# A routed-expert block on one core: the second routing chain moved to the front of the last stage, places by running sums, six shared blocks first, half-block sums at the end

## The chip, the core and the metric

The kernel runs on one core of a Trainium2 chip. The metric is the device time of one execution in microseconds (us), the median of several runs. The engines are named PE (matrix products), DVE (vector), ACT (activations), POOL (GpSimd) and SP (the queue that issues most transfers).

## What is computed

The input is x of 4096 tokens by 256. One attention layer (16 heads, causal, layer norm and modulation ahead of it) is added to x. Then a layer of experts follows, whose input h is the normalised, modulated x. In short form:

```python
logits = xf @ gate_w.T; scores = sigmoid(logits); sfc = scores + gate_bias
g_scores = top_k(sfc.reshape(n, 4, 4), 2)[0].sum(-1)      # 4 groups of 4 experts
gmask = the 2 best groups of each token
topk_idx = the 4 best experts among these groups; topk_w = their scores / sum * 2.5
y = einsum('nei,ne,ehi->nh', silu(xf@Wg) * (xf@Wu), cw, Wd)   # 16 experts, I = 128
shared = silu(xf @ Ws_g.T) * (xf @ Ws_u.T) @ Ws_d.T           # width 256
x = x + gb * (xf + y + shared)
```

Each token goes to exactly two groups, and in each group the kernel computes all four experts, with weight 0 for those not chosen.

## The kernel before

Four stages follow one another, each a block of code that all engines enter together: `prepare` and `attend` (the attention, about 1.65 ms), `project` (output projection, layer norm, router logits, from about 1655 to 1763 us) and `experts` (from 1763 us on).

**Routing.** Tokens are handled in two halves of 16 tiles of 128 (QT = 16). For each half a chain of small DVE instructions runs: `choose` (L1113) finds the two best groups (`mask`, kept as `chosen`) and the expert weights; `count_places` (L1168) lets PE count, by products with a triangular matrix (`earlier`) and a matrix of ones (`every`), how many earlier tokens chose each group, 17 products in all; `place_rows` (L1178) turns the counts into a row of a list for each token and group. `tile_table` (L1191) then works out which group each of the 19 tiles of 512 rows belongs to. Each instruction of a chain waits for the one before. The first half's chain runs inside `project`, one or two instructions at a time between the others (`route`); the second half's chain runs at the start of `experts`.

**Lists.** POOL sends each token's row (normalised input, 16 weights, slot numbers, 1104 bytes) to its two lists in memory by indirect transfers of 128 rows (`scatter`, L1216): 32 for the first half, then, once `s_rows` says the second half's places are there, 32 more.

**The last stage.** `experts` works through a list of jobs: 8 shared blocks S0 to S7 (512 tokens each, two items, one per half of the shared width) and 19 routed tiles R0 to R18 (512 list rows each, four items, one per expert). With FIRST_S = 4 the order is S0 to S3, R0 to R18, S4 to S7. An item is 12 products `up` (L1477) into hg and hu, ACT's silu (`sg`, L1549), DVE's product (L1652), ACT's rounded high part `ahi` (L1553), DVE's remainder `alo` (L1656), and 6 products `down` (L1495) into ya. Around them, per job: PE turns the rows (`turn`, L1443), ACT takes the high part (`high`, hhi, L1529), DVE the remainder (`low`, hlo, L1572); at the end ACT collects ya into z (`collect`, L1538), PE turns it back (`back`, L1458) and DVE takes it (`take`: L1607 for a shared block, L1610 into yo for a tile, which POOL then sends to `yr` by four indirect transfers, L1402). turn, back and the turning of the weights share one PSUM tile `tp`, whose uses have a fixed order, the list `uses`; the counting of places uses it too, as ("L", 0). For shared blocks DVE also runs `begin` (L1595, L1599: the row is gated and the residual added), which overwrites the row that POOL sent, and so waits for `s_sent`. For tiles, the weights of each expert come back from memory, broadcast (`cwb`, L1341), and DVE multiplies hu by them (L1649).

**Order around the change.** SP's queue issues the loads in program order. `load_tile(0)` waits for all scatters to have landed and for `begin` of the last leading shared block (`s_pre`). At the end, the two list results of each token (`yr`, 2 KB per token) are loaded by blocks (`load_pair`, 1 MB each, two buffers in turn: the space of cwb and that of wst) and added by DVE (`combine`, L1616 and L1618), three times inside the shared blocks S5 to S7 and five times after them; each finished block is stored (512 KB, `store`).

## Time and profile before

| | |
|---|---|
| median of 3 runs | 2344.61 us |
| lowest, highest of them | 2327.98, 2355.11 us |
| profiled execution, its own time | 2361.33 us |
| its span in the trace | 2359.1 us |
| PE busy in the span | 2107.5 us, 89% |
| DVE busy | 1763.8 us, 75% |
| ACT busy | 1421.5 us, 60% |
| POOL busy | 503.0 us, 21% |
| mean granted clock of PE | 0.93 |

Times in the text are from the start of the span. A row of the timeline gives the start, the duration, the engine, the line and the operation, output and inputs, the count, and in brackets how long the engine had been idle before it and what released it ("issue": nothing that the profile shows; "remote": a source that the profile doesn't know). A row of the windows view gives the stretch, its length, the busy time and count of each engine, PE's granted clock (1.00 is 2.4 GHz), the busy share of the 16 DMA engines and the GB/s moved. A row of the chain gives start, duration and the piece of work that the next piece waited for.

### The profile page before, as it was taken

The page shows a single profiled execution, that of the slowest core. Times are in us where ns is not written, and L with a number is a line of the kernel's source. Part 1 is how long each engine was busy: PE and PEld are TensorE (multiplying, and loading weights), DVE is VectorE, ACT ScalarE, POOL GpSimd, SP SyncE. Part 2 cuts the span into 40 slices and gives each one's busy share as a digit, 9 for nine tenths or more (in the row PEclk, how much of TensorE's full clock was granted, in tenths as well). Part 3 has the DMA queues.
Part 4 walks back from the last instruction along what each step waited for, and adds up shares of the span by engine and source line. Part 5 has one row for each costly group of instructions (what it writes and reads, how often), then busy time and mean ns, then how long its engine had stood idle before and what let it go on. Part 6 is the DMA issues. An engine that isn't in the chain of part 4 may idle for free. (4 is left out here: it accounts for less than half of the span.)

```text
span 2359.1 us, 43618 instructions
## 1 busy us (share of the span) xinstructions
PE 2107.5 (89%) x17400; PEld 1107.4 (47%) x17400; DVE 1763.8 (75%) x2226; ACT 1421.5 (60%) x2766; POOL 503.0 (21%) x756
## 2 busy tenths in 40 slices
PE   7589999999999999999999999999873689999994
PEld 5233333443444444344444333333573467777773
DVE  6478799999998878899999787764564346566666
ACT  5235577788888877778888888887210233333331
POOL 2000001110111001111101100000416446666640
PEclk9757799999999999999999999999765799999997
DMA  6815011114211111511101110000642233333326
GB/s 228 231 28 84 24 33 38 36 61 60 60 51 43 34 41 44 87 31 52 47 29 40 61 36 23 13 11 2 225 180 101 83 94 112 111 110 98 102 89 231
DMA packets 120685, 180.76 MB, mean 77 GB/s; under 512 B 15665, under 2 KB 80178, under 8 KB 119714
## 3 DMA queue, kind: packets, MB, share of 16 engines
q1 hardware_dynamic: 111776, 154.45, 23.2%
q0 software_dynamic: 6720, 19.01, 2.2%
q10 hardware_dynamic: 1986, 4.51, 0.5%
q8 instruction: 137, 2.24, 0.4%
q14 instruction: 66, 0.54, 0.1%
HBM read 99.92 MB, written 77.60 MB: 75 GB/s over the span
## 5 line engine op out<-in xcount | busy, mean ns | idle before, releaser
L775 DVE TENSOR_REDUCE mx<-S 128x2 f32<-128x1024 f32 (+3 forms) x1152 | 1279.3, 1134 | 200.3 <-PE S L688 127.0
L756 ACT ACTIVATE prob<-ST 128x512 f32<-128x512 f32 (+3 forms) x2304 | 1168.6, 559 | 353.4 <-PE ST L709 308.5
L723 PE MATMUL O<-prob,V 128*17 128x256 f32 (+1 forms) x8704 | 687.7, 389 | 0.3 <-POOL prob L666 0.3
L688 PE MATMUL S<-K,Q 48*128 48x512 f32 (+3 forms) x2304 | 570.2, 493 | 33.3 <-DVE mx L775 22.1
L709 PE MATMUL ST<-Q,K 49*128 49x512 f32 (+3 forms) x2304 | 491.9, 423 | 36.4 <-ACT prob L756 30.9
L688 PEld LDWEIGHTS S<-K,Q 48*128 48x128 f32 x2304 | 223.7, 191 | 472.0 <-issue 300.4
L666 POOL TENSOR_SCALAR_AFFINE_SELECT prob<-prob 128x512 f32<-128x512 f32 x128 | 81.2, 635 | 1208.1 <-ACT prob L756 1208.1
L709 PEld LDWEIGHTS ST<-Q,K 49*128 49x128 f32 x2304 | 223.7, 190 | 137.8 <-ACT prob L756 104.9
L723 PEld LDWEIGHTS O<-prob,V 128*17 128x17 f32 x8704 | 145.6, 96 | 287.1 <-issue 277.9
L1553 ACT ACTIVATE ahi<-sg 128x512 fp32r<-128x512 f32 x92 | 58.2, 632 | 192.5 <-DVE sg L1652 191.6
L1549 ACT ACTIVATE sg<-hg 128x512 f32<-128x512 f32 x92 | 55.4, 603 | 184.1 <-PE hu L1477 159.9
L1656 DVE TENSOR_TENSOR alo<-sg,ahi 128x512 fp32r<-128x512 f32 x92 | 82.5, 897 | 68.1 <-ACT ahi L1553 62.9
L1649 DVE TENSOR_TENSOR hu<-hu,cwb 128x512 f32<-128x512 f32 x76 | 53.1, 699 | 87.8 <-PE hu L1477 44.1
L1477 PE MATMUL hg<-hhi,wst 128*128 128x512 f32 x304 | 110.3, 404 | 0.0
L1495 PE MATMUL ya<-ahi,wst 128*128 128x512 f32 x304 | 109.8, 402 | 0.0
L1477 PE MATMUL hu<-hhi,wst 128*128 128x512 f32 x304 | 106.0, 389 | 0.0
L1402 POOL DMA_INDIRECT yr<-yo,idt x76 | 75.5, 993 | 41.1 <-DVE yo L1610 26.1
L1652 DVE TENSOR_TENSOR sg<-sg,hu 128x512 f32<-128x512 f32 x92 | 63.1, 686 | 21.4 <-ACT sg L1549 9.4
L694 PE MATMUL S<-maskh,idh 64*128 64x128 bf16 x1024 | 78.4, 234 | 0.0
L1219 POOL DMA_INDIRECT lists<-big,rows x64 | 63.0, 985 | 56.7 <-issue 46.3
L1386 POOL CAST wst<-whi 128x512 fp32r x76 | 47.4, 624 | 98.9 <-PE hu L1477 98.1
L1458 PE MATMUL tpe<-identf,z 128*128 128x128 f32 x216 | 30.4, 287 | 37.8 <-DVE hlo L1572 36.6
(235 smaller groups left out, 1804.8 us busy)
## 6 DMA issues: line engine op xcount, KB each, us to landing
cwb<-cwt SPq DMA_DIRECT2D x76, 256.0 KB, 5.3
lists<-wbd SPq DMA_DIRECT2D x132, 138.0 KB, 2.2
Q<-qs SPq DMA_DIRECT2D x192, 64.0 KB, 2.4
xs<-lists SPq DMA_DIRECT2D x19, 552.0 KB, 4.0
K<-ks SPq DMA_DIRECT2D x18, 512.0 KB, 15.3
qs<-hl SPq DMA_DIRECT2D x16, 512.0 KB, 4.3
ks<-hl SPq DMA_DIRECT2D x16, 512.0 KB, 4.2
wraw<-in_wcat SPq DMA_DIRECT2D x54, 128.0 KB, 2.1
```

The costliest lines, as they stand in the source:

```text
L666: pool.affine_select(out=tri, in_=tri, compare_op=ALU.is_ge, fill=0.0, base=0, pattern=[[0, HG], [1, P]], channel_multiplier=-1).then_inc( ...
L688: ins = pe.matmul(out[:, ab, 0:w], Q[g, n % QR, p, r * P:(r + 1) * P], K[G % 2][g, p, c * BW:c * BW + w], start=True, stop=not diag)
L694: ins = pe.matmul(out[:, ab, r * P:(r + 1) * P], idh[g, h, :], maskh[g, h, :], start=False, stop=h == 1)
L709: pe.matmul(ST[(u + ab) % ST_BANKS][:, c0:BW], K[G % 2][g, p, k * P:(k + 1) * P], Q[g, n % QR, p, c0:BW], start=True, stop=True).then_inc( ...
L723: ins = pe.matmul(O[32 * a:32 * a + VC, c0:c1], V[:, G, k, VC * a:VC * (a + 1)], prob[:, s % NP, a, c0:c1], start=s in FIRST and h == 0, s ...
L756: act.activation(prob[:, s % NP, 2 * p + ab, c0:BW], ST[u % ST_BANKS][:, c0:BW], ACT.Exp).then_inc(s_exp, 1)
L775: dve.tensor_reduce(mx[:, n % 2, a:a + step + 1:step, c], S[slot % S_RING][:, :, 0:w], AX_X, ALU.max).then_inc(s_free, 1)
L1402: pool.indirect_dma_start(d["yr"], bass.IndirectOffsetOnAxis(ap=idt[:, r % 4, i:i + 1], axis=0), yo[:, i, :], None).then_inc(s_sc, 16)
L1477: ins = pe.matmul(bank[:, :], w[:, c0:c0 + I], h[:, q % 2, half, :], start=(m == 0), stop=(m == 5))
L1495: ins = pe.matmul(ya[:, half, :], w[:, half * P:(half + 1) * P], a[:, it % 2, :], start=(k == 0 and m == 0), stop=(last and m == 2))
L1652: dve.tensor_tensor(sg[:, it % 2, :], sg[:, it % 2, :], up, ALU.mult).then_inc(s_pr, 1)
L1656: dve.tensor_tensor(alo[:, it % 2, :], sg[:, it % 2, :], ahi[:, it % 2, :].bitcast(F32), ALU.subtract).then_inc(s_act, 1)
```

## The change

- `count_places` issues two products instead of 17: one gives the count within a tile of 128, one the sum of each tile. `place_rows` forms the running sums of these on DVE in four steps (a copy and an addition each), adds the carry, and keeps the next carry; `choose` no longer sums the mask, and signals it right after its comparison.
- In `experts` the second routing chain comes first on DVE and PE: DVE runs `choose` and `place_rows`, then low(0), then `tile_table`, then low(1); PE counts the places before it turns S0. The use ("L", 0) of `tp` stands first, so turn(0) waits until `place_rows` is done.
- FIRST_S is 6: S0 to S5, R0 to R18, S6, S7.
- ACT rounds the next job's rows (`high(q+1)`) before it collects the results of the last job (`collect(q-1)`).
- `combine` and `load_pair` work on half blocks (2 tiles of 128, 512 KB), with six buffers in turn instead of two (cwb twice, wst three times, yo once), and all 16 halves are summed after the last `take`.

```diff
@@ choose
-    yield dve.tensor_scalar(mask, grank, float(TG) - 0.5, None, ALU.is_lt)
-    yield dve.tensor_reduce(r["added"], mask.rearrange("p t e -> p e t"), AX_X, ALU.add)
-    dve.tensor_tensor(r["carry"][:, g + 1, :], r["carry"][:, g, :], r["added"], ALU.add).then_inc(s_mask, 1)
+    dve.tensor_scalar(mask, grank, float(TG) - 0.5, None, ALU.is_lt).then_inc(s_mask, 1)
+    dve.wait_ge(s_mask, 1)
...
@@ count_places
-    pe.matmul(out, r["earlier"], mask, start=True, stop=False)
-    for i in range(1, QT):
-        pe.matmul(out[:, i * NG:QT * NG], r["every"], mask[:, 0:(QT - i) * NG], start=False, stop=False)
-    return pe.matmul(out.rearrange("p (t e) -> p t e", e=NG), r["every"],
-                     r["carry"][:, g, :].unsqueeze(1).broadcast_to([P, QT, NG]), start=False, stop=True)
+    pe.matmul(out[:, 0:QT * NG], r["earlier"], mask, start=True, stop=True)
+    return pe.matmul(out[:, QT * NG:2 * QT * NG], r["every"], mask, start=False, stop=True, skip_group_check=True)
@@ place_rows
-    yield dve.tensor_tensor(place, places.rearrange("p (t e) -> p t e", e=NG), r["first_row"], ALU.add)
+    yield dve.tensor_copy(a, sums)
+    step = 1
+    while step < QT:
+        dve.tensor_copy(b[:, 0:step, :], a[:, 0:step, :])
+        yield dve.tensor_tensor(b[:, step:QT, :], a[:, step:QT, :], a[:, 0:QT - step, :], ALU.add)
+        a, b = b, a
+        step *= 2
+    carry = r["carry"]
+    dve.tensor_tensor(carry[:, g + 1, :], carry[:, g, :], a[:, QT - 1, :], ALU.add)
+    yield dve.tensor_tensor(place, within, r["first_row"], ALU.add)
+    yield dve.tensor_tensor(place[:, 1:QT, :], place[:, 1:QT, :], a[:, 0:QT - 1, :], ALU.add)
+    if g:
+        yield dve.tensor_tensor(place, place, carry[:, g, :].unsqueeze(1).broadcast_to([P, QT, NG]), ALU.add)
...
-FIRST_S = 4
+FIRST_S = 6
+HALVES = 2 * NB
...
-    uses = [("T", 0)]
+    uses = [("L", 0), ("T", 0)]
...
-        yab = [cwb[:, :, :], wst[:, 0:TPB * 2 * D].bitcast(F32).rearrange("p (i n) -> p i n", i=TPB)]
+        yab = [cwb[:, 0:2, :], cwb[:, 2:4, :]]
+        yab += [wst[:, i * 4 * D:(i + 1) * 4 * D].bitcast(F32).rearrange("p (i n) -> p i n", i=2) for i in range(3)]
+        yab += [yo[:, :, :].rearrange("p i n -> p (i n)").rearrange("p (i n) -> p i n", i=2)]
+        ring = len(yab)
...
@@ sync engine
-                load_pair(0)
-                load_pair(1)
-                load_block(FIRST_S + 2)
+                for h in range(ring):
+                    load_pair(h)
                 for b in range(NB):
+                    for h in range(2 * b + ring, min(2 * b + ring + 2, HALVES)):
+                        load_pair(h)
                     store(b)
...
@@ tensor engine
+                need("mask", s_mask, 1)
+                count_places(pe, t, 1, counted).then_inc(s_tp, 1)
                 need("w0", t["s_w"][0], 16 * 4)
                 turn(0)
...
@@ scalar engine
                     if k == 0:
+                        if 0 < q < len(jobs) - 1:
+                            high(q + 1)
                         if q:
                             collect(q - 1)
-                        if 0 < q < len(jobs) - 1:
-                            high(q + 1)
...
@@ vector engine
-                low(0)
-                low(1)
                 for ins in choose(dve, t, 1, s_mask):
                     link(ins)
...
-                        if kind == "S" and x > FIRST_S:
-                            combine(combined)
-                            combined += 1
                 take(len(jobs) - 1)
-                for b in range(combined, NB):
-                    combine(b)
+                for h in range(HALVES):
+                    combine(h)
```

DVE at the start of the last stage, before (hlo is low(0) and low(1), cwb the space of the routing chain):

```order
L1563 UNCONDITIONAL_BRANCH
L1572 TENSOR_TENSOR hlo<-tpe,hhi 128x512 x4
L1118 MEMSET cwb 128x16 x4
L1120 TENSOR_TENSOR cwb<-cwb 128x256
L1125 TENSOR_TENSOR cwb<-cwb 128x16x8
```

And after the change, where the chain has given its rows (L1197, L1198) and the table begins (L1205):

```order
L1194 TENSOR_REDUCE cwb<-cwb 128x16
L1195 TENSOR_TENSOR cwb<-cwb 128x16
L1197 CAST rows<-cwb 128x16
L1198 CAST rows<-cwb 128x16
L1577 TENSOR_TENSOR hlo<-tpe,hhi 128x512 x2
L1205 TENSOR_TENSOR cwb<-cwb 128x32
```

low(0) has moved from before the chain to behind its rows, and low(1) to behind the table.

ACT at the first item of a job, before (hhi is the rounding of the next rows, z the collected results):

```order
L1553 ACTIVATE ahi<-sg 128x512
L1538 ACTIVATE z<-ya 128x512 x2
L1529 ACTIVATE hhi<-tpe 128x512 x2
L1549 ACTIVATE sg<-hg 128x512
L1553 ACTIVATE ahi<-sg 128x512
```

And after the change, at the same place:

```order
L1558 ACTIVATE ahi<-sg 128x512
L1534 ACTIVATE hhi<-tpe 128x512 x2
L1543 ACTIVATE z<-ya 128x512 x2
L1554 ACTIVATE sg<-hg 128x512
L1558 ACTIVATE ahi<-sg 128x512
```

The two pairs have changed places; nothing else moved on ACT but the order of the jobs.

SP's queue at the end, before (xs<-x loads the residual of a shared block, yr holds the list results):

```order
L1317 DMA xs<-x 128x4x256 x2
L1348 DMA cwb<-yr 128x4x512
L1348 DMA wst<-yr 128x4x512
L1317 DMA xs<-x 128x4x256
L1353 DMA out<-big 128x4x256
L1348 DMA cwb<-yr 128x4x512
L1317 DMA xs<-x 128x4x256
```

And after the change:

```order
L1329 DMA xs<-x 128x4x256 x2
L1360 DMA cwb<-yr 128x2x512 x2
L1360 DMA wst<-yr 128x2x512 x3
L1360 DMA yo<-yr 128x2x512
L1360 DMA cwb<-yr 128x2x512 x2
L1365 DMA out<-big 128x4x256
L1360 DMA wst<-yr 128x2x512 x2
```

Six half-block loads now stand in a row, and no residual load stands between the pairs.

## Rows read from the trace of the kernel before

**Rows 1.** Windows of the last stage.

```profile
1763.00:1814.00 51.00, 20.84 (x76) 17.71 (x76) 16.87 (x95) 4.16 (x6) 31.15 (x32) 0.57 0.28 99
1899.00:2288.00 389.00, 361.17 (x1745) 294.22 (x1746) 232.61 (x340) 137.31 (x246) 230.25 (x364) 0.99 0.33 103
2332.50:2359.00 26.50, 0.00 (x0) 0.00 (x0) 12.55 (x11) 0.00 (x0) 0.00 (x0) 0.53 0.81 272
```

**Rows 2.** Timeline of PE near the end of project: counting, then the last turn.

```profile
1746.39 0.67 PE L1171 MATMUL gl<-cwb 128*128 128x64 f32 x2
1746.85 6.51 PE L1173 MATMUL gl<-cwb 128*128 128x60 f32 x30
...
1753.68 1.91 PE L1053 MATMUL tpx<-identf,big 128*128 128x128 f32 x8
```

**Rows 3.** Timeline of DVE from the end of project into the last stage.

```profile
1747.27 1.67 DVE L1005 SCALAR_TENSOR_TENSOR big<-big,rstd,modB 128x256 f32<-128x256 f32 x4
...
1773.87 0.16 DVE L1118 MEMSET cwb<- 128x16 f32 x4
...
1779.98 1.17 DVE L1148 MAX8 cwb<-cwb 128x8 f32<-128x16 f32 x14
...
1788.02 0.11 DVE L1150 MEMSET cwb<- 128x64 f32 x1 [5.52 <-remote]
...
1808.97 0.17 DVE L1152 MATCH_REPLACE8 cwb<-cwb 128x16 f32<-128x16 f32 x1 [0.61 <-issue]
...
1814.38 0.17 DVE L1188 CAST rows<-cwb 128x16 int32<-128x16 f32 x1
...
1858.59 1.22 DVE L1607 TENSOR_TENSOR big<-big,tpe 128x1024 f32<-128x1024 f32 x1 [13.36 <-remote]
```

**Rows 4.** Timeline of POOL: first and last scatter of each half.

```profile
1763.83 1.23 POOL L1219 DMA_INDIRECT lists<-big,rows  x1 [27.39 <-issue]
...
1803.47 0.96 POOL L1219 DMA_INDIRECT lists<-big,rows  x1 [0.30 <-issue]
1814.88 0.96 POOL L1219 DMA_INDIRECT lists<-big,rows  x1 [10.46 <-DVEq L1634]
...
1855.23 0.96 POOL L1219 DMA_INDIRECT lists<-big,rows  x1 [0.30 <-issue]
```

**Rows 5.** Timeline of PE: first down of the stage, and turn(R0).

```profile
1822.89 0.80 PE L1495 MATMUL ya<-ahi,whi 128*128 128x512 f32 x1 [31.02 <-DVE alo L1656]
...
1876.80 1.97 PE L1443 MATMUL tpe<-identf,xs 128*128 128x128 f32 x8 [3.62 <-DMA xs<-lists]
```

**Rows 6.** Chain of waits at the first tile.

```profile
1873.03 3.72 DMA xs<-lists
```

**Rows 7.** Chain of waits within one routed tile.

```profile
1916.93 1.07 ACT z L1538 x2
1917.99 0.49 ACT hhi L1529
1918.51 0.52 DVE hlo L1572
```

**Rows 8.** Waits of back (L1458), 1890 to 2280 us: total, times.

```profile
  DVE hlo L1572: 29.6, 18
```

**Rows 9.** Timeline of PE: turn(S5) and turn(S6) near the end.

```profile
2283.66 1.03 PE L1443 MATMUL tpe<-identf,big 128*128 128x128 f32 x8
...
2294.43 1.04 PE L1443 MATMUL tpe<-identf,big 128*128 128x128 f32 x8
```

**Rows 10.** Timeline of SP: the first pair load.

```profile
2298.73 0.39 SPq L1348 DMA_DIRECT2D cwb<-yr  x1
```

**Rows 11.** Windows: pair loads, residual load and store together.

```profile
2306.00:2314.00 8.00, 2.78 (x13) 1.95 (x12) 6.00 (x8) 3.06 (x6) 0.00 (x0) 0.98 0.99 319
```

**Rows 12.** Timeline of DVE: the last block's sum; page, part 3: an instruction queue.

```profile
2353.36 1.23 DVE L1616 TENSOR_TENSOR big<-big,wst 128x1024 f32<-128x1024 f32 x1 [2.62 <-DMA wst<-yr]
...
q14 instruction: 66, 0.54, 0.1%
```

67 lines of the change are left out of this document (29 added, 38 removed).

## Prediction

> **What bounds the kernel now.** I first read the slices and the windows by stage, to see where PE is not busy. The change touches only the end of `project` and `experts`. There the windows show three different regimes: a start in which PE is busy 20.8 of 51 us [rows 1], a long middle of routed tiles in which it is busy 361 of 389 us, and a tail of 26.5 us after the last product, in which DVE is busy 12.6 us and the DMA engines 81% [rows 1].
>
> For the start I read the timelines of DVE, POOL and PE side by side. POOL sends 32 scatters at 1.28 us each (31 steps from 1763.83 to 1803.47), then sits idle 10.5 us until the second half's rows are there at 1814.4, and sends 32 more, 1.30 us each, until 1856.2 [rows 3, 4]. The routing chain of the second half starts on DVE at 1773.87, since low(0) and low(1) come first, and takes 40.7 us to its rows at 1814.55. Most of that is not work: it stops at 1781.15 and is back to its pace only at 1808.97 [rows 3]. In these 27.8 us DVE issues 26 small instructions, 1.07 us each, some of them with no wait in them at all. The same happens in the second run of scatters: `take` of S0 starts at 1858.59 after 13.4 us of waiting for nothing that the profile knows, 2.4 us after the last scatter [rows 3, 4]. So in both runs DVE comes nearly to a halt some 17 to 20 us after the scatters begin, and is freed 2.4 to 4.5 us after they end. I call this the standstill. It makes PE wait 31.0 us ahead of its first `down` [rows 5]. What ends last at the start is then this: R0's rows are loaded at 1873.03, land 3.7 us later, and turn(R0) runs at 1876.80 [rows 5, 6]. That time is the milestone of the start.
>
> For the middle I followed the chain of waits: in a tile it goes through z, then hhi, then hlo, then back [rows 7]. `back` waits for hlo 18 times, 29.6 us, 1.64 each [rows 8]. For the tail I read SP's queue and DVE: pair loads begin at 2298.73, when the last rows have been sent, and the last sum starts at 2353.36, after waiting for its load [rows 10, 12].
>
> All sums are made against the profiled execution, 2361.3 us (span 2359.1 and 2.2 around it). The median of the runs shown is 16.7 lower, and I carry that over at the end. A measurement of this kernel can tell about 1%, 23 us, from no change.
>
> **End of project.** Counting takes PE from 1746.39 to 1753.68, 7.3 us for 17 products; two of them take 0.67 [rows 2]. The turn behind it needs DVE's last rows, which end at 1748.94 [rows 3]. The chain's steps shift by two slots, so a long one (16 MATCH_REPLACE) moves ahead of the rows of block 6, which delays PE there, but DVE's total up to the rows of block 7 stays. I put the last turn at 1749.4 instead of 1753.68: **4.3 us** off, bounds 2 and 4.8. The 11 added instructions of `place_rows`, about 0.25 us each, run on DVE while PE does the last logits, and cost nothing as long as they take less than those 7 us. The stage then starts at about 1758.6.
>
> **Start of the last stage.** The chain starts at once. Without the standstill its length is 40.7 less 27.8, 12.9 us, plus about 3 for the sums: rows at about 1758.6 + 0.4 + 16 = 1775. This is just before the standstill would begin, 17 to 20 us after the first scatter at 1759.5. In either case the rows are there long before POOL has sent the first half, so POOL's pause of 10.5 us goes: 64 scatters, 82.5 us, from 1759.5 to 1842, landed at 1844.4 (2.4 more, by the release of DVE). R0's rows can then be at turn(R0) 1.1 (my estimate for SP, from its last wait to the issue) and 3.7 us later [rows 6], **1849.2**, if the shared blocks are through by then.
>
> Are they? turn(0) waits for the rows now. Before, the table, `begin` and the first item's products on DVE and ACT stood 8.3 us between the rows and the first `down` [rows 3, 5]; now the turn (1.9 [rows 2]), its rounding and an `up` come into it, and I put the first `down` 17 us behind the rows, at 1792. A shared block takes PE 10.8 us [rows 9], and turn(R0) stands in S5, four and three quarter blocks behind: 1843 if nothing stands still. Then POOL, not PE, decides, and two more shared blocks are done under it.
>
> With a standstill it is otherwise. POOL never pauses now, so it would last from about 1778 to 1844, 66 us, over nearly all of the 64 us of work that the blocks need. I bound its price from both sides. By the first one, 1.07 us per DVE instruction, 66 us let 61 through: 20 for low(0), the table and low(1), and 2 to 3 blocks of 10 by the code, 16 with separate waits; 15 to 28 us of work are left, and turn(R0) comes between 1859 and 1872. By the second one, the share of time: 26 instructions that take about 0.09 us each (14 in 1.17 [rows 3]) are 2.3 us of work in 27.8, and the later halt lets none through in 13.4; 6 of 64 us get done, 58 are left, and turn(R0) comes at 1902. Neither row is nearer, so I take the middle of 1866 and 1902, **1884**, 7 us later than before, but with six blocks done instead of four.
>
> What the standstill is, no row says. The Trainium skill ("Runtime: NRT & Kernel Launch", Instruction fetch mechanics) says that each engine's instruction store is refilled in blocks of 16 KiB while it executes, mostly hidden. If a late refill were the cause, the place in the program would decide and not the time since the scatters began; the chain has moved in the program, so by that rule the standstill could be gone. The trace has an instruction queue with 66 packets of together 0.54 MB, 8 KB each [rows 12], so its blocks are smaller than the page says, and two halts of different length at two places, each ending with the scatters, speak more for the scatters [rows 3, 4].
>
> **Routed tiles.** hhi now starts when ahi is done instead of after z, 1.07 us earlier [rows 7]. hlo's first half is then held by alo, and z ends where hhi ended before, so `back` comes about 0.9 us earlier, and is released by z and hlo together. The holes before `back` are 1.64 us on average and only one or two are below 0.9, so nearly all of it counts: 19 tiles, 0.8 each, **15 us**. The loop behind it (weights stored, broadcast back, hu, sg, ahi) starts at PE's own pace, so it moves along. Bounds: 0 (another wait, the broadcast of the weights, fills the hole) and 17.
>
> **End.** Take turn(S5) at 2283.66 as X. In the new order S7's turn stands there, with S6 and S7 left instead of S4 to S7. The rows of R18 are sent in the same way, and pair loads start at X+15. The last take ends at about X+21.7: one block less than 2294.43+10.8 plus the end of an item. Before the change the span ended at X+75.4. Now 8 MB are loaded and 4 MB stored after X+15. The best rate that mixes loads and stores is 319 GB/s in the windows view, with DMA at 99% [rows 11]; 12.6 million bytes at this rate are 39 us, at the 272 of the tail [rows 1] 46. DVE needs less: 32 additions of half the 1.23 us [rows 12], with their waits 22 us, and six buffers keep the loads coming. After the last load stand an addition and a store, 4 us. The end is at X+57 to X+64 (1 us of those 4 lies in the transfer time already). The old tail's pace says the same as the later one: 5 blocks in 26.5 us [rows 1], so 8 in 42 behind X+21.7. **15 us** off, bounds 10 and 20.
>
> **Sum.** +7 (which contains the 4.3) -15 -15 = -23 us in the profiled execution, 2338; less 16.7, **2321**.
>
> **Rivals.** (a) No standstill after the change, by whatever cause: turn(R0) at 1849 instead of 1877, -28, and -30 for the rest: 2303, less 16.7: **2287**. For it: the chain itself just escapes; 3 runs spread over 27 us, and the lowest is 33 below the profiled one, as if some runs had less of it. Against it: two of two runs of scatters had it.
>
> (b) The standstill is total and decides: no progress from 1778 to 1844, then 64 us of work, with a release 5 us late and the first one and a half blocks at PE's lower clock (0.57 in the first window [rows 1]; there eight turns take 1.91 us, later 1.03 [rows 2, 9], so a block takes some 9 us more): 1844+5+64+14=1927, +50; with -30 that is +20: 2381, less 16.7: **2365**, slower than before. It decides from turn(R0) later than about 1907.
>
> (c) The tile loop takes nothing, because `back` now waits for z instead of hlo, or for the weights: +7 -15 = -8, **2337**. For it: z ends hardly earlier than hlo did. Against it: both ends move by 0.9.
>
> **Chances.** Forecast, with a standstill as before, 0.5; (a) 0.28; (b) 0.1; (c) 0.12. The range goes from 2278 (a, with the end at its better bound) to 2354 (turn(R0) at 1902, and the smaller bounds elsewhere). Faster by over 1% (below 2321): all of (a) and half of the forecast: 0.54. Slower (above 2368): part of (b): 0.09. Within: 0.37.
>
> **What would show it.** In the profile after: (1) the stage starts at about 1758.6, with two counting products ahead; (2) the rows' CAST at about 1775, and POOL's 64 scatters without a pause until 1842; (3) gaps on DVE and ACT marked issue or remote between 1778 and 1844, which is the forecast, or none, which is (a); turn(R0) near 1884, 1849 or beyond 1907; (4) the wait of `back` for hlo or z down from 1.64 to about 0.8 us, and a period of a tile of 19.6 instead of 20.5; (5) DMA over 90% busy from the first pair load to the last store, ending 57 to 64 us after S7's turn. The forecast is wrong if turn(R0) is outside 1855 to 1905, or if the period or the tail don't shrink.

## The result and the profile after

The changed kernel takes 2337.7 us (median of 20 runs, 2315.0 to 2361.1); the kernel before takes 2348.9 (20 runs, 2328.0 to 2368.0). The ratio is 0.9942, 95% interval [0.9914, 0.9970]: 0.6% faster, which is within the 1% that was called no change. The forecast was 2321, with a range of 2278 to 2354; the gain came out at about half of the forecast one. The profiled execution after takes 2337.97 us (span 2335.7), 23.4 less than the one before.

To compare: in the 20 runs of the changed kernel the time falls by 1.72 us for each 0.001 of the run's mean granted clock (0.914 with 2361.1, 0.941 with 2315.0), and only 2.5 us of spread is left about that line. So beside medians I give times **at clock 0.93**, each run moved along that slope and averaged; for the changed kernel 2336.6. The profiled run of before (2361.3 at 0.929) is 2359.6 by that measure, 7 above the 2352 that its kind gives below; the profiled run after (2338.0 at 0.926) is 2331.1, 5.5 below its own kind. So two profiles differ by more than the kernels do.

The windows of the last stage after the change, columns as in [rows 1]:

```profile
1797.00:1849.00 52.00, 7.03 (x18) 5.26 (x18) 5.20 (x7) 3.70 (x5) 38.39 (x42) 0.53 0.31 111
1849.00:1904.00 55.00, 45.03 (x217) 37.08 (x218) 34.66 (x42) 20.21 (x36) 0.00 (x0) 0.90 0.15 49
1904.00:2285.00 381.00, 372.26 (x1801) 302.31 (x1800) 249.56 (x350) 143.05 (x254) 235.62 (x370) 0.99 0.34 108
...
2309.00:2336.00 27.00, 0.00 (x0) 0.00 (x0) 18.19 (x28) 0.00 (x0) 0.00 (x0) 0.50 1.00 361
```

Three things are to be seen. From 1797 to 1849 TensorE is busy 7 of 52 us, VectorE 5 and ScalarE 4, while GpSimd is at its scatters. In the tiles TensorE is now busy 98% of the stretch (93% before). In the last 27 us the DMA engines are full at 361 GB/s (81% and 272 before).

The timeline of PE, the two milestones of the start (answers to [rows 5]), then the timeline of POOL, the scatters around the half (answers to [rows 4]):

```profile
1781.02 1.94 PE L1452 MATMUL tpe<-identf,big 128*128 128x128 f32 x8 [15.18 <-DVEq L1637]
...
1789.66 1.34 PE L1452 MATMUL tpe<-identf,big 128*128 128x128 f32 x8
...
1839.22 0.80 PE L1504 MATMUL ya<-ahi,whi 128*128 128x512 f32 x1 [45.42 <-DVE alo L1660]
...
1903.45 1.97 PE L1452 MATMUL tpe<-identf,xs 128*128 128x128 f32 x8 [5.21 <-DMA xs<-lists]
```

```profile
1800.57 0.96 POOL L1229 DMA_INDIRECT lists<-big,rows  x1 [0.30 <-issue]
1801.84 0.96 POOL L1229 DMA_INDIRECT lists<-big,rows  x1 [0.31 <-issue]
...
1842.13 0.96 POOL L1229 DMA_INDIRECT lists<-big,rows  x1 [0.30 <-issue]
```

POOL's pause of 10.5 us is gone and the 64 scatters end at 1843, as forecast. But the first `down` comes at 1839.22 where 1792 was forecast, and turn(R0) at 1903.45, 26.7 us later than before. The timelines of DVE and ACT say where the time went:

```profile
1787.19 0.36 DVE L1213 TENSOR_SCALAR tile_g<-cwb 128x19 f32<-128x19 f32 x1 [1.17 <-DVE cwb L1212]
1787.90 0.19 DVE L1214 TENSOR_SCALAR tile_unit<-tile_g 128x19 int32<-128x19 f32 x1 [0.35 <-issue]
...
1792.79 0.23 DVE L1218 TENSOR_REDUCE cwb<-cwb 128x19 f32<-128x76 f32 x1 [4.47 <-issue]
1793.50 0.18 DVE L1219 TENSOR_TENSOR cwb<-cwb 128x19 f32<-128x19 f32 x1 [0.48 <-DVE cwb L1218]
1794.89 0.27 DVE L1220 TENSOR_SCALAR cwb<-cwb 128x19 f32<-128x19 f32 x1 [1.21 <-DVE cwb L1219]
1796.29 0.18 DVE L1221 SCALAR_TENSOR_TENSOR cwb<-cwb 128x19 f32<-128x19 f32 x1 [1.13 <-DVE cwb L1220]
1798.39 0.17 DVE L1223 TENSOR_SCALAR tile_row<-cwb 128x19 int32<-128x19 f32 x1 [1.92 <-remote]
1822.82 0.69 DVE L1577 TENSOR_TENSOR hlo<-tpe,hhi 128x512 fp32r<-128x512 f32 x1 [24.26 <-issue]
1834.02 0.69 DVE L1577 TENSOR_TENSOR hlo<-tpe,hhi 128x512 fp32r<-128x512 f32 x1 [10.51 <-issue]
...
1851.63 0.69 DVE L1656 TENSOR_TENSOR sg<-sg,hu 128x512 f32<-128x512 f32 x1 [12.47 <-ACT sg L1554]
```

```profile
1783.00 0.60 ACT L1534 ACTIVATE hhi<-tpe 128x512 fp32r<-128x512 f32 x1 [0.26 <-PE tpe L1452]
1822.19 0.60 ACT L1534 ACTIVATE hhi<-tpe 128x512 fp32r<-128x512 f32 x1 [38.59 <-remote]
1833.39 0.60 ACT L1534 ACTIVATE hhi<-tpe 128x512 fp32r<-128x512 f32 x1 [10.61 <-issue]
...
1850.93 0.60 ACT L1554 ACTIVATE sg<-hg 128x512 f32<-128x512 f32 x1 [12.49 <-remote]
```

This is the standstill, nearly total from 1788 on. What ScalarE needed for the second job's hhi (TensorE's second turn, done at 1791) was there 31 us before it ran. With the gaps of 10.6 and 12.5 us behind it, ahead of work whose inputs had been there as well (TensorE was through with its second `up` at 1793.8), ScalarE stands still for 54 of the 60 us from 1791 to 1851. VectorE stands still by itself only up to 1798, in its table. Its later gaps, of 24.3, 10.5 and 12.5 us, each end within 0.1 us of a result of ScalarE that it waits for: low(1) needs hhi, although the profile writes "issue" there. Between 1787 and 1798 the starts that are not back to back lie 0.70 us apart, or twice or three times that (0.71, 0.71, 1.39, 1.40, 2.10 in the rows above). It is over some 8 us after the last scatter; then the shared blocks follow at 10.1 us each.

In the tiles, 19 of them take 363.2 us from turn(R0) to the first shared block behind them, 19.1 each where they took 387.6, 20.4 each. The end, SP's first pair loads and the last store, and the window from there:

```profile
2299.97 0.91 SPq L1360 DMA_DIRECT2D cwb<-yr  x2
...
2327.63 4.28 SPq L1365 DMA_DIRECT2D out<-big  x2
```

```profile
2300.00:2336.00 36.00, 3.02 (x16) 1.90 (x14) 24.11 (x35) 1.17 (x3) 0.00 (x0) 0.58 0.97 350
```

With X the turn of the second shared block behind the tiles, S5 in the old order and S7 in the new one (2283.66, now 2284.9), pair loads begin at X+15, as forecast, and the span ends at X+50.8 where it ended at X+75.4.

So the 23.4 us are made up of +26.7 at the start, -25.4 from turn(R0) to X and -24.6 behind it. All three missed their forecast sizes, the start the other way from the other two.

### The profile page after: what moved, and what is told of

It reads as the page before. It is cut to its first block and busy times, and to the rows that moved or that the text cites. A ratio compares the mean times of both kernels' runs of the same rounds, so it can differ in the third digit from the quotient of the medians.

```text
span 2335.7 us, 43533 instructions
## 1 busy us (share of the span) xinstructions
PE 2091.1 (90%) x17338; PEld 1091.6 (47%) x17338; DVE 1778.7 (76%) x2260; ACT 1424.3 (61%) x2766; POOL 505.9 (22%) x756
## 5 line engine op out<-in xcount | busy, mean ns | idle before, releaser
L709 PE MATMUL ST<-Q,K 49*128 49x512 f32 (+3 forms) x2304 | 491.9, 423 | 35.7 <-ACT prob L756 30.2
L1660 DVE TENSOR_TENSOR alo<-sg,ahi 128x512 fp32r<-128x512 f32 x92 | 93.2, 1013 | 68.4 <-ACT ahi L1558 60.8
L1534 ACT ACTIVATE hhi<-tpe 128x512 fp32r<-128x512 f32 x54 | 29.4, 588 | 77.3 <-remote 38.6
```

The costliest lines, as they stand in the source:

```text
L709: pe.matmul(ST[(u + ab) % ST_BANKS][:, c0:BW], K[G % 2][g, p, k * P:(k + 1) * P], Q[g, n % QR, p, c0:BW], start=True, stop=True).then_inc( ...
L1660: dve.tensor_tensor(alo[:, it % 2, :], sg[:, it % 2, :], ahi[:, it % 2, :].bitcast(F32), ALU.subtract).then_inc(s_act, 1)
```

## The experiments

Each group of runs is one chip at one sitting, with the kernel before run beside it. Labels with `u_` undo one part of the change, `s_` and `c_` look into the standstill, `v_` are versions meant to be faster. "Start" is the time from the first scatter to turn(R0) in the profile: 113.0 before (four shared blocks first), 142.6 after (six). A label with a `b` at its end, or c_after2, repeats the kernel of the label without it in another group.

**Group 1: one part undone at a time** (before: 2352.2 at clock 0.93, 22 runs). Losses are against the changed kernel's 2336.6; it did not run in this group, and a repeat of it in group 5 gave 2334.3, so they are good to some 2 or 3 us.

```
+                        if q:
+                            collect(q - 1)
                         if 0 < q < len(jobs) - 1:
                             high(q + 1)
-                        if q:
-                            collect(q - 1)
```

> The changed kernel with ScalarE's old order: it collects the unit before ahead of rounding the next rows (high). Theory A: this order alone made the 19 tiles shorter (19.1 us each where they took 20.4), so undoing it gives 20.4 us per tile, the wait of back grows from about 0.4 to 1.5 us again, and the time is 24 us above the changed kernel's, start and end unchanged. Rival B: the tiles also gained from something else (six blocks first, or places of instructions in memory), then the period stays below 20.0 and the loss is under 15 us, the size that the forecast had for the order.

Measured: 2357.9 us median of 10, ratio 0.9995 [0.9951, 1.0039]; 2353.3 at clock 0.93, all of the gain gone. The period of a tile is 19.85 us (377.1 for 19), and waits of `back` for hlo are back: 18.8 us, 17 times, where the changed kernel has 4.6 us, 9 times, for z (before: [rows 8]). Start 143.5. The profiled run had a mean clock of 0.905, but in its tiles the granted clock is 0.99, as in the other profiles. The period is in B's range, the loss of 16.7 us between A's 24 and B's 15. The order is worth 13.9 us over the tiles in the profiles, about what the forecast said. For B's other gain there is no sign: the period of 20.4 us in the profile of before seems high for the old order, since the kernel before with pauses (s_pause_before, below) has 19.92, and waits of `back` for hlo of 20.1 us where the profile of before has 28.8 over its tiles.

```
-        yab = [cwb[:, 0:2, :], cwb[:, 2:4, :]]
...
+        yab = [cwb[:, :, :], wst[:, 0:TPB * 2 * D].bitcast(F32).rearrange("p (i n) -> p i n", i=TPB)]
...
-                for h in range(HALVES):
-                    combine(h)
+                for b in range(NB):
+                    combine(b)
```

> The changed kernel with the end in whole blocks again: two buffers of one block in place of six of half a block; still all sums after the last take, six shared blocks first. Theory A: the half blocks and the deeper ring are what took 24.6 us out of the end, which then goes back from X+50.8 to about X+70, some 20 us longer in all. Rival B: the end is bound by the transfer of the pairs and by VectorE's sums, which are the same in whole blocks, so the end is X+55 to X+60 and the loss is 5 to 9 us; the rest of the gain came from where the first pair load stands and from no sums between the last shared blocks. Start and tiles unchanged under both.

Measured: 2342.9 us median of 7, ratio 0.9956 [0.9918, 0.9994], 2343.0 at clock 0.93: 6.4 lost. The end is X+61.3; the last sum waits for its load as in [rows 12]:

```profile
2332.71 1.23 DVE L1618 TENSOR_TENSOR big<-big,wst 128x1024 f32<-128x1024 f32 x1 [2.79 <-DMA wst<-yr]
2333.97 1.23 DVE L1620 TENSOR_TENSOR big<-big,wst 128x1024 f32<-128x1024 f32 x1
```

B is nearer: the half blocks are worth 10.5 of the 24.6 us of the end in the profile. The rest belongs to the end without block loads and block sums between the pairs and with two blocks fewer; no run undid these by themselves.

```
-FIRST_S = 6
+FIRST_S = 4
...
                 for h in range(ring):
                     load_pair(h)
+                load_block(FIRST_S + 2)
+                load_block(FIRST_S + 3)
```

> The changed kernel with four shared blocks first in place of six; two more shared blocks at the end, their loads behind the six half-pair loads. Theory A (the standstill sets the start, and the blocks behind it are paid at 10.1 us each wherever they stand): turn(R0) at 1883 in place of 1903.5, tiles unchanged, X 0 to 2 us earlier or later, the end at X+50 or somewhat less since the half pairs are loaded by then; total within 5 us of the changed kernel. Rival B: six blocks first is a gain of its own, since block loads beside tile work or pair loads at the end cost: 10 us or more slower. Rival C: turn(R0) stays near 1900, because the routed part waits for the scatters, and the total is 15 us or more slower.

Measured: 2351.8 us median of 10, ratio 0.9959 [0.9923, 0.9994], 2344.6 at clock 0.93: 8.0 lost. Start 121.2, 21.4 less: A is right there, the blocks behind the standstill cost what they cost anywhere. The loss is B's: the block loads now stand behind six pair loads. In DVE's timeline `begin` of S6 waits for its load, and in PE's a `back` then waits for what follows on VectorE and ScalarE:

```profile
2314.41 1.22 DVE L1606 TENSOR_TENSOR big<-big,xs 128x1024 f32<-128x1024 f32 x1 [9.47 <-DMA xs<-x]
```

```profile
2319.03 1.30 PE L1469 MATMUL tpe<-identf,z 128*128 128x128 f32 x5 [9.02 <-ACT z L1545]
```

From the first shared block behind the tiles to the end it takes 101.5 us; v_mix below, also with four blocks first but with these loads further ahead, takes 84.6. So that is a loss of the place of these loads more than of the number of blocks.

```
+                low(0)
+                low(1)
                 for ins in choose(dve, t, 1, s_mask):
...
                         turn(q + 1)
+                        if q == 0:
+                            need("mask", s_mask, 1)
+                            need("tpf", s_tpf, use_of[("L", 0)])
+                            count_places(pe, t, 1, counted).then_inc(s_tp, 1)
```

> The changed kernel with the second routing chain behind the first two low() of VectorE, and its counting matmuls behind turn(1) on TensorE, as before the change (counting still by two matmuls and running sums). Theory A: VectorE and ScalarE nearly stop while scatters follow one another, whatever their program order; the chain then falls into that stretch: its rows are ready near 1810, the scatters pause about 10 us and end near 1855, and turn(R0) comes at 1895 to 1903, so the moved chain gained nothing or cost up to 8 us. Rival B (the recorded argument): the early chain spares about 7 us, so undoing it puts turn(R0) at 1910 or later.

Measured: 2329.3 us median of 4, ratio 0.9876 [0.9837, 0.9916], 2334.0 at clock 0.93. POOL pauses 13.1 us ahead of the second half and its last scatter starts at 1851.0, and turn(R0) still comes 137.5 us after the first scatter, 5.1 earlier than with the early chain. A holds: with the standstill the early chain gains nothing; in the profile it costs 5 us, and the 2.6 us by the times are no more than the groups differ by.

**Group 2: pauses, and a mixed version** (before: 2350.2 at clock 0.93, 13 runs).

```
                                     t["xe"][:, n, :], None).then_inc(t["s_sent"][n // TPB], 16)
+        if n % TPB == TPB - 1:
+            pool.wait_ge(t["s_sent"][n // TPB], 16 * TG * TPB)
```

> The changed kernel with GpSimd waiting after every 8 scatters until their rows have landed (a pause of about 2.5 us, 7 more in all, 20 us). If the standstill builds up over many scatters in a row (it began 10 us after the first), pauses let VectorE and ScalarE catch up: the shared blocks run beside the scatters and turn(R0) comes at 1862 + 10 to 20 us, no later than without pauses. If it is there whenever a scatter is being written, the pauses add their 20 us: turn(R0) 160 us after the first scatter, and the kernel 15 to 20 us slower.

Measured: 2308.3 us median of 4, ratio 0.9853 [0.9779, 0.9926], 2310.6 at clock 0.93. That is 26 under the changed kernel's 2336.6 of another group; by the distance to before in its own group, 39.6 us against the changed kernel's 15.6, it is 24. Start 105.0: no standstill, and TensorE has finished all six blocks and waits 25.6 us for R0's rows. The pauses are in POOL's timeline, the wait in PE's:

```profile
1770.85 0.96 POOL L1229 DMA_INDIRECT lists<-big,rows  x1 [0.30 <-issue]
1773.61 0.95 POOL L1229 DMA_INDIRECT lists<-big,rows  x1 [1.80 <-DMA lists<-big,rows]
```

```profile
1794.60 0.51 PE L1506 MATMUL ya<-ahi,whi 128*128 128x512 f32 x1 [3.24 <-DVE alo L1662]
1866.64 1.75 PE L1454 MATMUL tpe<-identf,xs 128*128 128x128 f32 x7 [25.62 <-DMA xs<-lists]
```

```
+COMBINED = [(NB - 2, 1), (NB - 1, 0), (NB - 1, 1)]
...
+                load_block(FIRST_S + 2)
+                load_pair(0)
+                load_pair(1)
+                load_block(FIRST_S + 3)
+                for h in range(2, ring):
+                    load_pair(h)
...
+                    if kind == "S" and (x, k) in COMBINED:
+                        combine(COMBINED.index((x, k)))
```

> A version meant to beat both: the changed kernel with the chain and counting back behind the first two low() and turn(1), four shared blocks first, the last block's load put between the second and third half-pair load, and three half-block sums inside the last two shared blocks. From the undo runs: turn(R0) 117 us after the first scatter (before 113, changed kernel 142.7), tiles at 19.1 us, and an end of 84 to 90 us from turn of the first shared block behind the tiles (before 94.7; changed kernel 69.1 with two blocks fewer, so 89.3 by like count). Total 5 to 8 us under the changed kernel. Rival: block loads and block sums beside the pair loads cost again what they cost in the run with four blocks first (101.4 us), then it is no faster than the changed kernel.

Measured: 2329.0 us median of 10, ratio 0.9910 [0.9869, 0.9950], 2330.9 at clock 0.93, 5.7 under the changed kernel's 2336.6 and 19.3 under before in its own group, 3.7 more than the changed kernel in its own. Start 116.7, with the standstill (TensorE waits 40 us ahead of its first `down`), in the same group in which the run with pauses had none; the end 84.6 from the first shared block behind the tiles. Start and end are as expected, the total by the first of the two counts only (5 to 8 were expected). Its edit takes that of u_late with it.

**Group 3: what the scatters move, and pauses elsewhere** (before: 2337.2 at clock 0.93, 13 runs).

```
-            pool.indirect_dma_start(d["lists"], bass.IndirectOffsetOnAxis(ap=t["rows"][:, n, k:k + 1], axis=0),
-                                    t["xe"][:, n, :], None).then_inc(t["s_sent"][n // TPB], 16)
+            pool.indirect_dma_start(d["short"], bass.IndirectOffsetOnAxis(ap=t["rows"][:, n, k:k + 1], axis=0),
+                                    t["xe"][:, n, D:XW], None).then_inc(t["s_sent"][n // TPB], 16)
```

> The changed kernel, no pauses, with scatters that move only the last 20 numbers of a row (80 bytes in place of 1104) into a table of their own; as many scatters, rows and semaphores. The rows' 256 leading numbers are left out of the tiles (read from the prefilled lists, one DMA more per tile), so only the stretch up to turn(R0) is compared. Theory A1 (the bytes in flight make VectorE and ScalarE stand still): the stretch from the first scatter to turn(R0) falls from 142.7 to 105 us or less, as with pauses. Theory A2 (what is queued per row or per scatter does, not the bytes): it stays at 135 to 143 us.

Measured: 2297.4 us, one run; start 91.9, no standstill.

```
-                scatter(pool, t, d, 0)
-                need("rows", s_rows, 1)
-                scatter(pool, t, d, 1)
...
+                            sp.dma_start(d["spare"][row:row + P, :], t["xe"][:, n, :]).then_inc(t["s_sent"][n // TPB], 16)
```

> The changed kernel with the 64 indirect scatters of GpSimd replaced by 64 direct DMAs of the same size from SyncE's queue into a spare table; the lists stay as prefilled, the tiles compute on empty rows, the end's sums read other rows of the same size, so again only the stretch up to turn(R0) counts. A2 (GpSimd's stream of indirect scatters): no standstill, the six shared blocks follow at 10.1 us each and turn(R0) comes 75 to 90 us after the start of the stage. A1 (bytes): it stays over 120 us. If it were the place of the instructions in the program, as the skill's fetch rule would have it, pauses could not have removed it; this run then shows nothing new.

Measured: 2280.6 us, one run; turn(R0) 85.7 us after the start of the stage, no standstill.

> The kernel before the change, with the same pauses after every 8 scatters. If the standstill cost it too: low(1) no longer late, four shared blocks done beside the scatters, the chain's rows at about 1788 in place of 1814, turn(R0) at about 1763.8 + 82 + 20 + 5, thus 107 us after the first scatter where it was 113; 5 to 8 us faster than before, and the whole change is worth 32 to 36 us with pauses where it was 15.6 without. Rival: before loses nothing by the standstill (its four blocks wait for the scatters anyway) and the pauses' own cost of some 20 us makes it slower or equal.

The edit is that of s_pause on the kernel before. Measured: 2333.9 us median of 10, ratio 1.0016 [0.9975, 1.0057], 2343.7 at clock 0.93, 6.5 over before; start 101.2, with TensorE waiting 38.8 us for R0's rows. This decides between neither theory, since before itself stood at 2337 here, and not at 2352.

```
-FIRST_S = 6
+FIRST_S = 8
...
-                load_block(FIRST_S)
-                load_block(FIRST_S + 1)
...
+        if n % TPB == TPB - 1:
+            pool.wait_ge(t["s_sent"][n // TPB], 16 * TG * TPB)
```

> A version meant to beat all so far: the changed kernel with the pauses and with all eight shared blocks ahead of the tiles. In the run with pauses TensorE stood still for some 26 us between the sixth block and turn(R0) at 1866.6; two blocks of 10.1 us fit there. turn(R0) 0 to 8 us later, since begin() of the last block must wait for the last scatters, and the end shorter by 18 to 20 us less what the pair loads, now without cover, need: in all 5 to 15 us faster than with pauses alone. Rival: the pair loads start 15 us after the last tile either way and nothing computes beside them, and VectorE's late begin() holds up the tiles, so it is the same within 3 us.

Measured: 2292.8 us median of 4, ratio 0.9814 [0.9724, 0.9904], 2307.9 at clock 0.93. Start 109.2 with eight blocks in it.

**Group 4: the changed kernel as a control** (before: 2337.2 at clock 0.93, 11 runs).

> The changed kernel itself, once more, beside the kernel before and the pause variants on one chip, since chips differ. The profiles of before and after differ by 23.4 us, the medians of 20 by 11.2. If the profile of before lay above its own kind (its tiles took 20.4 us each, the undo run of ScalarE's order 19.85), the difference of times at equal granted clock is 12 to 18 us here; if the profiles are typical it is 20 to 25 us.

Measured: 2288.3 us median of 6, ratio 0.9833 [0.9780, 0.9886], 2300.0 at clock 0.93. This was expected by no theory: the same kernel, 37 us faster at the same clock. Start 92.4; the timeline of PE shows the first `down` and turn(R0) where rival (a) of the prediction had them:

```profile
1782.60 0.79 PE L1504 MATMUL ya<-ahi,whi 128*128 128x512 f32 x1 [3.24 <-DVE alo L1660]
...
1843.13 1.97 PE L1452 MATMUL tpe<-identf,xs 128*128 128x128 f32 x8 [12.67 <-DMA xs<-lists]
```

So the standstill isn't a property of the kernel alone. Groups 3 and 4, with before at 2337, had none in any profile; group 1 and, without pauses, group 2, with before at 2350 to 2352, had it. That voids the readings of group 3 on bytes and direct DMAs.

```
+        if n % (2 * TPB) == 2 * TPB - 1:
+            pool.wait_ge(t["s_sent"][n // TPB], 16 * TG * TPB)
```

> The changed kernel with a pause after every 16 scatters in place of every 8 (3 pauses in all). In the changed kernel the first gaps of VectorE came 9 us after the first scatter, the long ones after some 30 us. If the standstill needs a long row of scatters to build up, pauses after 16 (every 21 us) clear it almost as well: turn(R0) at 97 to 105 us after the first scatter (105.0 with pauses after 8; 142.7 without). If 8 in a row is about the limit: 115 to 135 us.

Measured: 2297.2 us median of 4, ratio 0.9817 [0.9722, 0.9913], 2304.3 at clock 0.93; start 96.2. Without a standstill to remove, the pauses cost 4 us.

> The changed kernel with pauses after every 8 scatters and with the chain and counting back behind low(1) and turn(1). With the standstill gone, the second half's scatters are the bound: early chain, rows ready at 1779.3, scatters gapless; late chain, rows ready when the chain has run behind low(1), some 1763 + 30 = 1793, before the first half's scatters end at 1809. If so, the early chain is worth nothing with pauses either, and turn(R0) comes 103 to 106 us after the first scatter in both. Rival: with the late chain the rows are not ready by the end of the first half, the scatters wait, and turn(R0) is 5 us or more later: then moving the chain is worth something once nothing stands still.

Edits of s_pause and u_late together. Measured: 2292.0 us median of 4, ratio 0.9866 [0.9793, 0.9939], 2310.5 at clock 0.93; start 105.5 against 105.0 with the early chain. The early chain is worth nothing with pauses either.

**Group 5: the same questions beside a control with the standstill** (before: 2351.8 at clock 0.93, 7 runs).

> The changed kernel once more, as the control of this group. So far each group of runs (one chip, one sitting) was of one of two kinds: in some every kernel without pauses had the standstill (before about 2351 us at a granted clock of 0.93), in others none had (before about 2337, the changed kernel 2300 where it was 2337). turn(R0) at 140 us or more after the first scatter says that this group is of the first kind, at 92 us of the second. Theory S (a matter of the sitting): every kernel of this group without pauses, the one before the change too, is of the same kind as this one.

Measured: 2337.3 us median of 4, ratio 0.9892 [0.9845, 0.9939], 2334.3 at clock 0.93; start 142.2, TensorE waits 45.9 us ahead of the first `down`. It is of the first kind, and with before at 2351.8 and the next run theory S holds.

> The changed kernel with scatters of 80-byte rows (the rows' leading 256 numbers are left out of the tiles), again, beside a control. If the control has the standstill: turn(R0) at 92 us means that the bytes make it (A1), at 140 us that the stream of scatters does, whatever its bytes (A2). If the control has none, this run says nothing.

Measured: 2350.5 us, one run; start 143.0, against the control's 142.2. The timeline of PE, first `down` and turn(R0):

```profile
1834.74 0.80 PE L1507 MATMUL ya<-ahi,whi 128*128 128x512 f32 x1 [45.98 <-DVE alo L1663]
...
1899.10 1.11 PE L1455 MATMUL tpe<-identf,xs 128*128 128x128 f32 x4 [6.08 <-DMA xs<-lists]
```

A2: with a fourteenth of the bytes the standstill is the same to within 1 us.

> The changed kernel with 64 direct DMAs from SyncE's queue in place of the scatters (the tiles compute on empty rows, the end's sums read other rows), again, beside a control. If the control has the standstill: turn(R0) at 86 us after the start of the stage means that GpSimd's indirect scatters are needed for it, 120 us or more that the traffic alone makes it. If the control has none, this run says nothing.

Measured: 2255.4 us, one run at a clock of 0.953; turn(R0) 85.9 us after the start of the stage, at 1733.9 here. The same two rows, and those of SP's queue that stand in for the scatters:

```profile
1766.31 0.79 PE L1511 MATMUL ya<-ahi,whi 128*128 128x512 f32 x1 [3.23 <-DVE alo L1667]
...
1819.75 1.54 PE L1459 MATMUL tpe<-identf,xs 128*128 128x128 f32 x6 [5.19 <-DMA xs<-lists]
```

```profile
1733.76 16.59 SPq L1372 DMA_DIRECT2D spare<-big  x32
1750.39 0.62 SPq L1329 DMA_DIRECT2D xs<-x  x1
1751.07 16.19 SPq L1372 DMA_DIRECT2D spare<-big  x32
```

The same bytes go out in 34 us and not in 82, and nothing stands still. So the bytes alone don't do it, and the control beside it, with GpSimd's stream of indirect DMAs, has it. The run changes the queue, the kind of transfer and the length of the stream together, though, and the long gaps of the changed kernel begin only 27 us after the first scatter; which of the three spares it isn't shown.

> The changed kernel with 3 pauses (after every 16 scatters), in a group with its control. If the group has the standstill: with the pauses doing away with it, turn(R0) 96 us after the first scatter and 30 us faster than the control; if 8 in a row is about the limit, 115 us or more. If the group has none: 4 us slower than the control, as in the last group (2304.3 against 2300.0 at a clock of 0.93).

Measured: 2325.3 us median of 4, ratio 0.9860 [0.9806, 0.9913], 2331.6 at clock 0.93, 2.7 under the control. Start 136.5: most of the standstill is there, and here TensorE is hit too. Between 1803 and 1809 its matmuls, 0.39 us long and with their data in place, start 0.70 to 1.40 us apart:

```profile
1803.24 0.39 PE L1488 MATMUL hg<-hhi,wlo 128*128 128x512 f32 x1 [1.20 <-issue]
1804.64 0.39 PE L1488 MATMUL hg<-hhi,whi 128*128 128x512 f32 x1 [1.01 <-issue]
1805.34 0.40 PE L1488 MATMUL hg<-hlo,whi 128*128 128x512 f32 x1 [0.30 <-issue]
...
1807.50 0.54 PE L1488 MATMUL hu<-hhi,whi 128*128 128x512 f32 x1 [0.93 <-issue]
1808.90 0.59 PE L1488 MATMUL hu<-hlo,whi 128*128 128x512 f32 x1 [0.87 <-issue]
```

**Group 6: the best version where the standstill is** (before: 2354.4 at clock 0.93, 10 runs).

> The version with pauses after every 8 scatters and all eight shared blocks ahead of the tiles, once more, to see it in a group of the kind with the standstill. Before at a granted clock of 0.93 tells the kind: about 2351 us with, 2337 without. With: if pauses after 8 do away with it (as in the one run that had them in such a group, turn(R0) 105 us after the first scatter), turn(R0) comes 109 us after the first scatter as in its first run, and the kernel is at 2306 to 2312, 40 us under before and 25 under the changed kernel. If that run was only lucky: turn(R0) at 150 us or more. Without: 2308 at that clock again, some 8 us over the changed kernel's 2300.

Measured: 2299.3 us median of 6, ratio 0.9741 [0.9689, 0.9792], 2306.4 at clock 0.93. Start 110.2; TensorE goes from one shared block to the next and waits 7.7 us for R0's rows:

```profile
1804.49 0.79 PE L1504 MATMUL ya<-ahi,whi 128*128 128x512 f32 x1 [3.23 <-DVE alo L1660]
...
1881.63 1.75 PE L1452 MATMUL tpe<-identf,xs 128*128 128x128 f32 x7 [7.73 <-DMA xs<-lists]
```

Pauses after 8 do away with the standstill, in two groups that have it (this one by before's time alone). This version takes the same in both kinds of groups, 2307.9 and 2306.4, where the changed kernel takes 2300 or 2334 to 2337.

## Why the prediction came out as it did

**End of project.** From the first product of `project` (1667.48 before, 1668.71 after) to the last turn it takes 86.2 us before and 82.0 after: 4.2 less, forecast 4.3, with two counting products for each half. The first instruction of the last stage is at 1760.1, 2.9 earlier than before, because the stages ahead took 1.2 longer in this run.

**Start: the step that failed.** Rows' CAST at 1779.4 (forecast 1775), 64 scatters without a pause to 1843 (forecast 1842) and gaps from about 1770 on (forecast 1778): the mechanism, a standstill that lasts until the scatters end, was right. What failed is the price of the standstill: "Neither row is nearer, so I take the middle of 1866 and 1902, 1884". Measured 1903.5, just past the upper bound, the one that took the share of time of the first halt. The other bound, 1.07 us for each DVE instruction, came from the first halt, in which small instructions of VectorE still got through in steps of 0.70 us and multiples. It was a price for VectorE alone, and the work behind it was held up by ScalarE: 54 us of standing still with its inputs there, five instructions from 1798 to 1850, against VectorE's seven, of which the two low(1) waited for ScalarE. The halt that let nothing through (13.4 us) should have weighed more than the one that did. The term was +26.7 (turn(R0) at 1903.5 for 1876.8), not +7, in the profile, and rival (b), from 1907 on, was nearly the case. That the early chain helps under a standstill was a misreading as well: undone, the start was 5.1 us shorter. Nor does the running sum beat the matmuls there: with the late chain POOL pauses 13.1 us, before 10.5, which fits the 11 instructions more on DVE; that wasn't tried by itself.

**Whether it stands still at all.** Rival (a) happened too. In group 4 turn(R0) came 92.4 us after the first scatter, forecast 89.7 for that case. That the median there, 2288.3, is rival (a)'s 2287 is luck: it belongs to a clock of 0.9375, and at 0.93 it is 2300. The forecast looked for the cause in what the change does; whether the standstill comes lies outside the kernel. With it the change is worth 15.6 to 17.5 us at equal clock, without it 37.

**Tiles.** Forecast -15 by the order of `high` and `collect`. The order alone is worth 13.9 (u_order). That answers rival (c) as well: its time, 2337, is the measured one, but its mechanism, no gain in the tiles, is not what happened; `back` does wait for z now, 4.6 us in all. The profile showed -24.4 over the 19 tiles (-25.4 up to X), 10 more, because the tiles of the profiled run of before took 20.4 us and not the 19.9 of the two other runs with the old order. At equal clock the two profiled runs are 28.5 us apart and the kernels 15.6. The slow tiles can cover the 7 that before's run lies above its kind; for the 5.5 that the other lies below its own no row gives a cause. The medians differ by 11.2 only; the clocks of the runs of before in that comparison aren't recorded, so whether they explain the rest is open.

**End.** Forecast -15 (bounds 10 and 20), measured -24.6. Pair loads at X+15 is right. The sum's rate was too low: it took 319 GB/s from a window with a residual load in it [rows 11]; the new end runs at 350 over its 36 us and 361 in its last 27, and 12.6 million bytes take 35.7 us and not 39 to 46. The rest is that the last addition and store lie within those 35.7 us. That the end gets shorter was right; the half blocks are 10.5 of the 24.6.

**Sum.** -23 forecast in the profile and -23.4 found is luck: +19.7 too little at the start, 10.5 and 9.6 too little elsewhere. **Offset.** The 16.7 us taken off for the median was the profiled run's distance to a median of 3; to the median of 20 it was 12.4, and the profile after lies on its own median. In numbers this is the whole 17 us by which the forecast time missed: a profile's distance to its median doesn't carry over to another kernel's. It is so only because the errors of the three terms cancel in the profiles. Between the kernels they don't: with the tiles at the 13.9 of u_order the terms come to +26.7 -13.9 -24.6 = -11.8, and the medians differ by 11.2 (15.6 at equal clock) where 23 was forecast. The start, 20 us too cheap in the forecast, took about half of the gain. The range's upper end, 2354, doesn't come out of the bounds it names either: 25 more at the start, nothing from the tiles and 10 off the end make 2360.

**The place in the program.** The forecast weighed the place of the instructions as a cause and set it aside. The runs agree with that: the same program stood still in group 5 and not in group 4, and pauses on GpSimd, with the other engines' code as it was, removed it. One of the forecast's two reasons doesn't hold: beside the queue of 66 packets of 8 KB each, the page of before has a second instruction queue:

```profile
q8 instruction: 137, 2.24, 0.4%
```

That is 16 KB a packet, the size that the Trainium skill ("Runtime: NRT & Kernel Launch", Instruction fetch mechanics) states. Whether a refill that comes due while the scatters run is held up by them, no run tried.

## What to carry to other kernels

A long row of indirect DMAs on GpSimd can stop the other engines' issue, in some sittings and not in others: wait for the rows to land after every 8 (that cost 10 us where there was no standstill and gave 24 to 26 where there was) and put work that doesn't need them beside it. Compare versions only beside a control in the same group, and at equal granted clock: here a sitting moved the changed kernel by 37 us and the clock by 46, more than any edit. Price an unknown stall by its worst stretch and not by its mean, and for each engine on the path, not for the one on which it was seen first.

## What the runs showed of the hardware that was not expected

- The standstill comes with a row of indirect DMAs on GpSimd: not with direct DMAs of the same bytes from SyncE's queue, which are also sent in 34 us and not 82 (turn(R0) after 85.9 us), and as much with 80-byte as with 1104-byte rows (143.0 and 142.2). Pauses of mostly 1.8 us after 8 remove it (105.0), after 16 hardly (136.5).
- Which engine holds up the stage depends on the order of the work. In the changed kernel it is ScalarE: idle for 38.3 to 38.6, 10.6 and 12.5 us, at the same places in the first comparison, in c_after2 and in s_rows80b. With the chain behind low(0) and low(1) it is VectorE, in whose chain the halt then falls: ScalarE waits 46.5 us (before) and 48.6 us (u_late) for VectorE.
- It is a matter of the sitting: present in four groups (the first comparison, 1, 2, 5; and 6 by before's time), absent in two (3, 4). Neither chip nor kernel decides it: one chip had both kinds (groups 2 and 4), and the changed kernel had both. What does is open.
- While it lasts, many instructions start 0.70 us or a multiple of it after the one before, on VectorE and, in one run, on TensorE, with or without a semaphore to wait for.
- Where it is absent, GpSimd pays instead: 8 of the 64 scatters of group 4's control took 1.2 to 2 us in place of 0.96, against 1 in group 5's, and the 64 starts take 85.0 us against 80.2. That the engines contend for something then is argued, not shown.
